# Layer 0's 780 field pairs in six full tiles and a doubled half tile, instead of seven tiles of 117 and 78 rows

## What is computed

```
for idx, (W, b) in enumerate(params):       # W: (39, fk, 128), fk = 39, 64, 64
    z = einsum('bhd,bkd,hks->bsd', x0, xk, W) + b[None, :, None]
    z = relu(z)
    if idx != n_layers - 1:
        xk = z[:, :64, :]; direct.append(z[:, 64:, :])
    else:
        direct.append(z)
logit = sum(concatenate(direct, axis=1), axis=-1)      # (2048, 256)
h = relu(concatenate([logit, dense_ctx], 1) @ W_top1 + b_top1)
y = relu(h @ W_top2 + b_top2) @ W_top3
```

## Time and profile before

| | |
|---|---|
| time, median of 3 executions | 2402.55 us (2402.54 to 2406.84) |
| the profiled execution: its own time, its span | 2402.38 us, 2400.6 us |
| mean granted clock of TensorE | 0.994 |
| busy: PE, DVE, ACT, GpSimd | 97%, 94%, 54%, 83% |
| moved by DMA | 476.58 MB, mean 199 GB/s |

### The profile page before, as it was taken

How to read it: one execution, slowest core, us unless ns; L and a number is a source line. 1 busy time by engine, 2 the same in 40 slices (tenths; PEclk the granted TensorE clock), 3 DMA queues, 4 the chain that set the end, 5 groups by cost and what they waited for, 6 DMA issues and landing times.

```text
span 2400.6 us, 32500 instructions
## 1 busy us (share of the span) xinstructions
PE 2331.3 (97%) x7904; PEld 1495.3 (62%) x7904; DVE 2253.1 (94%) x2241; ACT 1305.2 (54%) x1534; POOL 2001.7 (83%) x1284
## 2 busy tenths in 40 slices
PE   2799999999999999999999999999999999999999
PEld 1466666666666666666666666666666666666656
DVE  3699999999999999999999999999999999999984
ACT  3355555555555555555555555555555555555553
POOL 5688988988898898898888889889888888988650
PEclk9899999999999999999999999999999999999999
DMA  8977877877887787787787788778778778877820
GB/s 200 203 180 214 234 180 206 229 191 198 222 214 186 212 229 180 209 233 185 201 224 203 194 215 223 183 210 232 181 203 229 200 194 217 214 186 213 235 70 10
DMA packets 404771, 476.58 MB, mean 199 GB/s; under 512 B 172241, under 2 KB 181457, under 8 KB 404369
## 3 DMA queue, kind: packets, MB, share of 16 engines
q1 hardware_dynamic: 304552, 310.24, 52.5%
q10 hardware_dynamic: 79722, 160.99, 21.9%
q0 software_dynamic: 20480, 5.15, 1.9%
HBM read 466.56 MB, written 9.71 MB: 198 GB/s over the span
## 4 chain that ended last, share of the span: by engine, by line
PE 95%; DMA 2%; POOL 1%; SPq 1%; ACT 0%; issue 0%; DVE 0%; ACTq 0%; DVEq 0%; POOLq 0%
PE z L733 93%; DMA xb<-x_rows 1%; DMA x_rows<-rows 1%; POOL rows L523 1%; DMA rows<-table,index 0%; SPq L434 0%; PE z L846 0%; PE z L848 0%; PE z L806 0%; PE z L851 0%; POOL low L554 0%; ACT high L900 0%; PE x L828 0%; PE prod_dve L828 0%; PE prod_dve L826 0%
## 5 line engine op out<-in xcount | busy, mean ns | idle before, releaser
L554 POOL TENSOR_TENSOR low<-prod_pool,high 128x1024 fp32r<-128x1024 f32 (+1 forms) x576 | 1379.9, 2396 | 212.9 <-ACT high L900 206.4
L733 PE MATMUL z<-prod_whole,w_whole 128*128 128x512 f32 (+2 forms) x2432 | 1129.1, 593 | 38.9 <-DVE prod_whole L609 38.9
L733 PE MATMUL z<-high,w_high 128*128 128x512 f32 (+1 forms) x1792 | 865.5, 483 | 26.8 <-ACT high L900 22.6
L900 ACT ACTIVATE high<-prod_pool 128x1024 fp32r<-128x1024 f32 (+1 forms) x576 | 611.0, 1061 | 406.9 <-DVE prod_pool L609 234.9
L733 PEld LDWEIGHTS z<-prod_whole,w_whole 128*128 128x128 f32 (+2 forms) x2432 | 460.8, 190 | 423.1 <-issue 361.4
L733 PE MATMUL z<-high,w_low 128*128 128x512 f32 (+1 forms) x1792 | 709.3, 396 | 0.0
L523 POOL DMA_INDIRECT rows<-table,index x640 | 610.5, 954 | 115.8 <-issue 98.2
L609 DVE TENSOR_TENSOR prod_pool<-xh,x 128x1024 f32<-128x1024 f32 x512 | 622.4, 1216 | 35.5 <-ACT x L878 32.8
L609 DVE TENSOR_TENSOR prod_whole<-xh,x 128x1024 f32<-128x1024 f32 (+1 forms) x576 | 615.4, 1096 | 6.1
L900 ACT ACTIVATE high<-prod_dve 128x1024 fp32r<-128x1024 f32 (+2 forms) x384 | 338.8, 882 | 482.2 <-DVE prod_dve L609 319.7
L733 PE MATMUL z<-low,w_high 128*128 128x512 f32 (+1 forms) x1664 | 553.6, 426 | 0.0
(11 more groups left out here) (52 smaller groups left out, 383.8 us busy)
## 6 DMA issues: line engine op xcount, KB each, us to landing
xh<-x_rows SPq DMA_DIRECT2D x63, 2560.0 KB, 17.7
xh<-x_rows ACTq DMA_DIRECT2D x63, 2432.0 KB, 19.1
xb<-x_rows SPq DMA_DIRECT2D x64, 546.0 KB
xb<-x_rows SPq DMA_DIRECT2D x62, 468.0 KB
xb<-x_rows SPq DMA_DIRECT2D x64, 312.0 KB
xa<-x_rows SPq DMA_DIRECT2D x190, 78.0 KB
xb<-x_rows SPq DMA_DIRECT2D x62, 234.0 KB
rows<-table,index POOLq DMA_INDIRECT x640
```

The source lines that it names most:

```text
L554: pool.tensor_tensor(low[0:g.rows, g.split_slot, 0:n, :], prod_pool[0:g.rows, g.slot, 0:n, :], high[0:g.rows, g.split_slot, 0:n, :].bitcas ...
L733: return pe.matmul(z[stage][:, :], weights[0:g.rows, table[stage, g.tiles[i]], :], src[0:g.rows, i, :], start=g.begins_layer and first, st ...
L900: act.activation(high[0:g.rows, g.split_slot, 0:n, :], src[0:g.rows, 0:n, :], ACT.Copy).then_inc(high_ready, 1)
```

## The change

Layer 0 gets six tiles of 128 rows. On partitions 117 to 127 (MORE = 11 rows) of tile t = 0 to 5 stand the pairs (i, i + 18 + t) for fields i = 0 to 10. For t = 0 and 1 these are shifts 18 and 19; those of t = 2 to 5 (shifts 20 to 23) are pairs that earlier shifts hold, and get zero weights. What is left of shifts 18 and 19, fields 11 to 38, is 28 x 2 = 56 rows, which stand twice in tile 6 (REST), on partitions 0 to 55 and 64 to 119, with zeros between: a half tile with two passes. Its first factor has a buffer of its own, `xa_rest`, in SBUF. `load_rest` adds six transfers on SP's queue: 11 rows of xa (22 KB), 11 x 6 rows of xb (132 KB), and four of 56 rows (112 KB each) for the half tile. The regular loads stop at tile 6, 39 rows less in each of two of them (78 KB each). DVE clears `xa_rest` and xb's tile 6 once at the start, and SP waits for that before its first load.

GROUPS changes in all three layers. The number of groups stays 26; there are ten instead of nine whose low parts are GpSimd's, and ten whole ones instead of eleven. The new one of GpSimd is tile 18 of layer 1 alone, the last group of that layer, so that its low pass is the layer's last.

```diff
-T0 = -(-SHIFTS // JT)
-LAST0 = (SHIFTS - JT * (T0 - 1)) * F
+T0 = SHIFTS // JT + 1
+REST = T0 - 1
+MORE, MORE_AT = 128 - JT * F, JT * REST
+LEFT_AT = MORE
+LEFT = F - LEFT_AT
...
-    0: [(WHOLE, 6, 1), (BY_DVE, 0, 2), (BY_POOL, 2, 2), (WHOLE, 4, 2)],
-    1: [(BY_DVE, HALF_TILE, 1), (BY_POOL, 0, 2), (WHOLE, 2, 2), (WHOLE, 4, 1), (BY_POOL, 5, 2),
-        (WHOLE, 7, 2), (BY_DVE, 9, 2), (BY_POOL, 11, 2), (BY_DVE, 13, 2), (BY_POOL, 15, 2),
-        (WHOLE, 17, 2)],
-    2: [(BY_POOL, 0, 2), (WHOLE, 2, 1), (WHOLE, 3, 2), (BY_POOL, 5, 2), (WHOLE, 7, 2),
-        (BY_DVE, HALF_TILE, 1), (BY_POOL, 9, 2), (BY_DVE, 11, 2), (BY_POOL, 13, 2), (WHOLE, 15, 2),
-        (WHOLE, 17, 2)],
+    0: [(WHOLE, 0, 2), (BY_DVE, REST, 1), (BY_POOL, 2, 2), (WHOLE, 4, 2)],
+    1: [(BY_DVE, HALF_TILE, 1), (BY_POOL, 0, 2), (WHOLE, 2, 2), (BY_POOL, 4, 2), (WHOLE, 6, 2),
+        (BY_DVE, 8, 2), (BY_POOL, 10, 2), (BY_DVE, 12, 2), (BY_POOL, 14, 2), (WHOLE, 16, 2),
+        (BY_POOL, 18, 1)],
+    2: [(BY_POOL, 0, 2), (WHOLE, 2, 2), (BY_DVE, 4, 2), (BY_POOL, 6, 2), (WHOLE, 8, 1), (BY_POOL, 9, 2),
+        (WHOLE, 11, 2), (BY_DVE, HALF_TILE, 1), (BY_POOL, 13, 2), (WHOLE, 15, 2), (WHOLE, 17, 2)],
...
-PAIR_PARTS = [(0, 0, T0), (1, 0, 4), (1, 4, T0), (2, 0, (SHIFTS - 2 + JT - 1) // JT)]
+PAIR_PARTS = [(0, 0, REST), (1, 0, 4), (1, 4, REST), (2, 0, REST)]
-X0_LOADS = JT + len(PAIR_PARTS)
+X0_LOADS = JT + len(PAIR_PARTS) + 6
...
-        self.half = stage > 0 and first == HALF_TILE
-        self.rows = 128 if stage else (LAST0 if first == T0 - 1 else JT * F)
+        self.half = first == (HALF_TILE if stage else REST)
+        self.rows = 128
...
+        def load_rest(engine, c):
+            of = rows_of(c)
+            step = of.ap[0][0]
+            engine.dma_start(xa[JT * F:128, :], of[0:MORE, :]).then_inc(x0_loaded, 16)
+            more = bass.AP(tensor=of.tensor, offset=of.offset + MORE_AT * step,
+                           ap=[[step, MORE], [step, REST], [1, CN]])
+            engine.dma_start(xb[JT * F:128, 0:REST, :], more).then_inc(x0_loaded, 16)
+            for at in (0, H):
+
+                first = bass.AP(tensor=of.tensor, offset=of.offset + LEFT_AT * step,
+                                ap=[[step, LEFT], [0, 2], [1, CN]])
+                engine.dma_start(xa_rest[at:at + 2 * LEFT, :], first).then_inc(x0_loaded, 16)
+                second = bass.AP(tensor=of.tensor, offset=of.offset + (LEFT_AT + MORE_AT) * step,
+                                 ap=[[step, LEFT], [step, 2], [1, CN]])
+                engine.dma_start(xb[at:at + 2 * LEFT, REST, :], second).then_inc(x0_loaded, 16)
...
                     wait_made(sp, 0, c - 1)
+                else:
+                    sp.wait_ge(rest_cleared, 2)
                 load_pairs(sp, c, PAIR_PARTS[:BY_SP] if c.known and c.n < 2 else PAIR_PARTS)
+                load_rest(sp, c)
...
+                    other = xa_rest if stage == 0 and g.half else shared
...
+            dve.memset(xa_rest[:, :], 0.0).then_inc(rest_cleared, 1)
+            dve.memset(xb[:, REST, :], 0.0).then_inc(rest_cleared, 1)
...
-                act.activation(xa_ps[0:JT * F, :], xa[:, :], ACT.Copy).then_inc(xa_copied, 1)
+                act.activation(xa_ps[:, :], xa[:, :], ACT.Copy).then_inc(xa_copied, 1)
```

More of the change, by code:

```diff
@@ L231, in tower @@
         xh = [sb(f"xh{i}", [128, TK, CN]) for i in range(2)]
-        xa = sb("xa", [JT * F, CN])
-        xb = sb("xb", [JT * F, T0, CN])
+        xa = sb("xa", [128, CN])
+        xa_rest = sb("xa_rest", [128, CN])
+        xb = sb("xb", [128, T0, CN])
         prod_whole = sb("prod_whole", [128, SLOTS[WHOLE], PAIR, CN])
@@ L319, in tower @@
         x0_loaded = sem("x0_loaded")
+        rest_cleared = sem("rest_cleared")
         xa_copied = sem("xa_copied")
@@ L608, in products @@
                     t = slice(g.tiles[0], g.tiles[0] + n)
+                    other = xa_rest if stage == 0 and g.half else shared
                     dve.tensor_tensor(
                         into[0:g.rows, 0:n, :], spread[0:g.rows, t, :],
-                        shared[0:g.rows, :].unsqueeze(1).broadcast_to([g.rows, n, CN]), ALU.mult,
+                        other[0:g.rows, :].unsqueeze(1).broadcast_to([g.rows, n, CN]), ALU.mult,
                     ).then_inc(products_ready, 1)
@@ L787, in chunk @@
                 contract(2, c)
-            pe.wait_ge(w_ready, sum(g.split for g in PLAN[0, 0]))
+            pe.wait_ge(w_ready, sum(g.split + g.half for g in PLAN[0, 0]))
             pe.wait_ge(w_rounded, len(GROUPS[0]))
@@ L1027, with place @@
     w0b = np.zeros((128, T0, S), w0.dtype)
-    first = np.arange(F)
-    for j in range(SHIFTS):
-        second = (first + j) % F
-        at = slice(j % JT * F, (j % JT + 1) * F)
-        w0a[at, j // JT] = w0[first, second]
-        if j:
-            w0b[at, j // JT] = w0[second, first]
+    placed = set()
+    def place(first, second, tile, *rows):
+        pair = frozenset((first % F, second % F))
+        if pair in placed:
+            return
+        placed.add(pair)
+        for row in rows:
+            w0a[row, tile] = w0[first % F, second % F]
+            if len(pair) == 2:
+                w0b[row, tile] = w0[second % F, first % F]
+    for j in range(JT * REST):
+        for f in range(F):
+            place(f, f + j, j // JT, j % JT * F + f)
+    for i in range(MORE):
+        for tile in range(REST):
+            place(i, i + MORE_AT + tile, tile, JT * F + i)
+    for k in range(LEFT):
+        for s in range(2):
+            place(LEFT_AT + k, LEFT_AT + k + MORE_AT + s, REST, 2 * k + s, H + 2 * k + s)
+    assert len(placed) == F * (F + 1) // 2
     def by_fields(w):
```

## The result

Changed kernel 2437.68 us (median of 4, 2425.04 to 2444.90), before 2402.93 us beside it: ratio 1.0135 [1.0092, 1.0179] (the two medians by themselves give 1.0145). Forecast were 2395.8 us and a range to 2405. The profiled execution has 2438.88 us and a span of 2437.1.

The account below looks back on a forecast made before the run. PE's passes were taken to bound the kernel between prologue and tail. From 2402.38 us, -14.3 (one pass less per chunk) +7 (prologue loads) +0.7 (PE in the prologue) gave 2395.8, range 2389 to 2405.

Parts of the forecast that it names:

- PE's work: Stage-0 passes of chunks 2 to 63: one fp32r pass less, 0.23 us per chunk, period 35.15, 14.3 us off.
- DVE's low part shrinks, 0.53 us off: DVE's layer 0: low part falls from 1.224 to 0.695 us per chunk, products staying three pairs and one single.
- GpSimd: One more low part, a single tile at the end of layer 1, taking 1.31 us; it still fits the period.
- so no wait in PE: End of layer 1: slack 1.1 us for GpSimd's new low part, 0.9 for layer 0's low(2,3) behind it.
- SP and its transfers: X0 loads grow from 7 to 13 per chunk, +446 KB (+25%); the six more issues fit, slack remains.
- 5 us or more of slack become about 3: Steady state: added x0 bytes at 209 GB/s or less take 2.2 to 3 us of the slack before xa's copy.
- The xh loads land 2 to 3 us later, a period before use: Steady state: xh loads behind the added x0 loads are delayed 2 to 3 us, still a period early.
- The prologue: Three chunks' added loads, 1.37 MB, lie on the chain: 7 us, ends 2 and 13.7; plus 0.7 for PE.
- C: Steady state: chunk loads over 5 us late hold ACT at xa's copy; 0.3 us per chunk, 2415; chance 0.04.
- A: Prologue takes nearly all: loads queue behind xh's at half rate, 13.7 plus 0.7 cancel 14.3; 2402.5; chance 0.29.
- B: End of layer 1: GpSimd's low(18) late for stage 1's last pass, 0.4 us per chunk, +25, 2420; chance 0.08.
- D: Steady state: the gain does not appear because DVE, at 98%, paces after all; +7, 2410; chance 0.03.

Follow-up runs that it names:

- x_none: Changed kernel without its six additional transfers, buffers cleared once instead; 2393.22 us, ratio 0.9964.
- b_plus56: Kernel before plus the four 56-row transfers per chunk, into two buffers that nothing reads; 2414.53 us, ratio 1.0044.
- x_early: Changed kernel with SP storing the next chunk's rows ahead of its wait for the sums instead of behind it; 2410.69 us, ratio 1.0029.
- b_early: Kernel before with SP's row stores moved ahead of its wait for the sums; 2403.62 us, ratio 1.0001.
- x_xa6: Changed kernel with ACT copying xa two groups later, after layer 1's tile 14 rounding instead of tile 10; 2734.35 us, ratio 1.1384.
- x_sep: Changed kernel with the four 56-row transfers on their own semaphore, waited for only by DVE's half product; 2753.69 us, ratio 1.1480.
- x_no56: Changed kernel without the four 56-row transfers, the two 11-row ones kept; 2401.11 us, ratio 0.9989.
- x_no11: Changed kernel without the two 11-row transfers, the four 56-row ones kept; 2404.36 us, ratio 1.0007.
- x_xhlate: Changed kernel with ACT issuing its xh load behind the copy of xa instead of ahead of layer 1's roundings; 2776.13 us, ratio 1.1557.
- b_xhlate: Kernel before with ACT's xh load moved behind the copy of xa; 2667.02 us, ratio 1.1100.
- x_os_early: Changed kernel with the 56 rows loaded once, on their own semaphore, and row stores ahead of SP's wait for the sums; 2401.85 us, ratio 0.9994.

## Why the prediction was wrong, step by step

**PE's work: the count right, its worth less than half.** 1600 passes with low operands, one fp32r pass less per chunk. What a period gains where the loads don't disturb is 35.37 - 35.27 = 0.10 us instead of 0.23, so 6 us instead of 14.3. The other 0.13 us are not fully explained. A likely part is the half product's turn at the port, a cost that "DVE's low part shrinks, 0.53 us off" had left out: the product was costed from a row with one factor in PSUM (0.68 us), and takes 0.69 to 1.46.

**GpSimd: the cost right, the deadlines missed.** The single low part takes 1.29 us (median of those in the middle), forecast 1.31. It fits, and x_none shows that it isn't the cause of the loss. But the prediction had a slack of 1.1 us for it and 0.9 for the low part behind it, "so no wait in PE"; in x_none PE waits for each of them in every other chunk, 0.26 and 0.36 us on average.

**SP and its transfers: here the prediction failed.** The step was "5 us or more of slack become about 3", from bytes over rate: +2.2 to 3 us. The landing moved by 4.9 us (13.3 to 18.2), and the slack went to zero. The rate was not the error: with as many bytes more, b_plus56 lands 2.5 us later than before, and x_early 2.7 later than b_early. What the step left out is what stands beside the loads and behind them. Thirteen issues alone take 8.0 us of SP (1035.84 to 1043.86), the four 56-row ones 0.8 to 0.9 us each and not the 0.35 of the earlier trace rows, so the last ones start as ACT's xh load does. "The xh loads land 2 to 3 us later, a period before use" failed likewise: they land 7.4 and 5.2 us later (17.7 to 25.1, 19.1 to 24.3). They have time before their own use, but they run into the next row stores, whose dependent issue moves from 4.3 to 5.2 us (median). That is in the loop, so a late chunk delays the next. x_none against the changed kernel prices the steady part: 0.46 us per chunk, 28 us. Why the same loads, once late, need 2 us more is shown only by where they stand: 7.9 us ahead of ACT's xh load they land in 18.2, 11.4 ahead of it (x_early) in 16.0, 3.9 and 3.6 ahead (x_xa6, x_sep) in 23.6 and 23.9.

**The prologue: direction right, size off.** Forecast +7, with 2 to 13.7 as ends; measured 118.3 to 132.4, +14.1, beyond the upper end by 0.4. ACT's copies of xa for chunks 0 and 2, before and after, show where it arose:

```profile
37.35 0.60 ACT L891 ACTIVATE xa_ps<-xa 117x512 f32<-117x512 f32 x1 [20.46 <-DMA xb<-x_rows]
116.89 0.60 ACT L891 ACTIVATE xa_ps<-xa 117x512 f32<-117x512 f32 x1 [13.58 <-DMA xb<-x_rows]
...
47.25 0.60 ACT L921 ACTIVATE xa_ps<-xa 128x512 f32<-128x512 f32 x1 [30.74 <-DMA xb<-x_rows]
130.94 0.60 ACT L921 ACTIVATE xa_ps<-xa 128x512 f32<-128x512 f32 x1 [18.31 <-DMA xb<-x_rows]
```

Chunk 0's copy comes 9.9 us later, chunk 2's 14.05: nearly 10 us arise with chunk 0's loads and some 4 more with chunk 2's. Scaling each chain step by +25% had given 3.2 and 5.0: chunk 2's was near, chunk 0's is the term that was mis-sized. The chain of after has the last step hardly longer than before, 20.21 us against 19.90, but starting 13.7 us later, and PE restarts behind it.

```profile
110.70 20.21 DMA xb<-x_rows
...
132.53 0.79 PE L763 MATMUL z<-high,w_high 128*128 128x512 f32 x1 [14.01 <-ACT high L930]
```

From x_none (116.0) the six loads take 16.4 us for three times 602 KB, which would be 113 GB/s, where 200 to 250 had been taken. The Trainium skill's figure for small transfers ("DMA: Bandwidth & Descriptors", section Bandwidth) had given an estimate of 13.4 us. The row of 209 GB/s was preferred to it; the measured 14.1 and 16.4 us stand nearer to the page. That is luck: by the same figure x_no56's 154 KB, three times, would be 3.4 us, as an estimate, and 6.9 were measured (116.0 to 122.9), while x_no11's 448 KB would be 10.0 and took 7.1. What sets the cost of chunk 0's loads stays open.

This term alone would have led out of the range: 2402.4 - 6 + 14.1 is 2410.5.

**The rivals.** C named the place and the path rightly (loads late at the copy of xa, roundings behind it) and had 2415 at a chance of 0.04: it counted a slack of 5 us that nothing else would eat. A had the prologue's size nearly right (13.7), but by bytes at half rate, which x_no56 and x_no11 speak against. B's place did become late, by 0.26 us in every other chunk and not 0.4 in each, and cost far less than its 25 us. D, DVE setting the pace, did not happen as told, though the gain came to less than half. The 2410.5 of the prologue as measured and the steady gain as realised is x_early's 2410.69, and the 28 us of the loads in the steady state make the rest of 2438.88: the account closes. C's remark that the loads fall on few DMA engines was not tried; no view here shows single ones.

## What to carry to other kernels

Before adding a transfer to a tuned stream, follow what lies behind it around the whole cycle: a store that waits in program order for a result, and a load that waits for that store, make a loop through DRAM, whose slack (5.3 us here, of 35.4) is the real budget. Bytes over rate priced the added loads well (2.5 to 2.7 us) as long as they ended ahead of the next stream. So count issues as well as bytes, and look which large transfer starts before the last of them has landed. Price a prologue from its own steps: chunk 0's loads there cost nearly 10 us where a share by bytes gave 3.2. When one more operand moves from PSUM to SBUF, ask which GpSimd operation stands beside it.

## What the runs showed of the hardware

- Row stores of 64-byte pieces took 4.3 us to the dependent issue at a DMA share of 0.30 (before, 1224 to 1229 us) and 12.6 us beside xh's loads, at 0.91 (x_xhlate, 1034 to 1047 us), for some 116 KB.
- The order of issues can latch (hold a slow cycle once it is in it): in x_xa6, x_sep, x_xhlate and b_xhlate the same work settled into a cycle of 39.7 to 41.1 us, where 35.4 was possible, with a granted clock of 0.95 to 0.96 in 400 to 2200 us (x_xa6, x_sep, x_xhlate), where PE was busy 90 to 91% of the time. x_sep and x_xa6 have ACT's xh load 3.6 and 3.9 us behind SP's first x0 issue, x_os_early 12.8; what moves it there in x_sep and x_xa6 was not followed up.
- The 56-row transfers, whose source is 28 rows times 2 for 56 partitions, took 0.79 to 0.94 us to issue (changed kernel, after 400 us), nearly three times the 0.3 of the others. The one of 11 partitions times 6 rows, whose source rows overlap too, took 0.30.
- A VectorE product with both factors in SBUF took 0.69 to 2.9 us for the same 64 or 128 x 512 elements, by what GpSimd was doing.
